# Graph network on one Trainium2 core: scatters without an index limit, and another order in the prologue

## What is computed

```
h = relu(layernorm(x))
hW = (h @ W.T) as 4 heads of 32;  att[e] = leaky_relu(a_src . hW[src] + a_dst . hW[dst], 0.2)
x = x + segment_sum(att[e] * hW[src], dst)                       # layer 0
h = relu(layernorm(x))
z = concat(h[src], h[dst], edge_attr)
x = x + segment_sum(relu(z @ W_weight + b) * sigmoid(z @ W_gate + b), src)   # layer 1
```

## Time and profile before

| | |
|---|---|
| median of 3 runs | 5451.1 us (5448.32 to 5451.26) |
| profiled execution, whole | 5452.95 us |
| profiled execution, first to last instruction | 5451.3 us |
| granted TensorE clock, mean | 0.897 |
| busy PE / DVE / ACT / POOL | 3900.8 / 3303.6 / 2039.0 / 3655.4 us |

### The profile page before, as it was taken

One profiled execution on the slowest core, in us unless ns is written; L12 is line 12 of the kernel. 1 busy time (PEld: TensorE's weight loads), 2 busy tenths in 40 slices (PEclk: granted clock), 3 DMA queues, 4 the chain that ended last, 5 costly groups with the idle time before them and its releaser, 6 DMA issues.

```text
span 5451.3 us, 120513 instructions
## 1 busy us (share of the span) xinstructions
PE 3900.8 (72%) x33107; PEld 3037.0 (56%) x33107; DVE 3303.6 (61%) x7367; ACT 2039.0 (37%) x4548; POOL 3655.4 (67%) x3908
## 2 busy tenths in 40 slices
PE   5666666666666656698778778877887775888882
PEld 4355555555555555466556556655665554666662
DVE  6999777777777777652222222222222226999996
ACT  4022222222222222353333333333333335888872
POOL 4677777777777777447777777777777774444441
PEclk8898888888888888899999999999999998999996
DMA  5233333333333332465555555555555558999998
GB/s 179 64 81 81 78 76 76 78 76 79 75 76 78 76 78 75 151 226 170 165 164 166 167 167 164 165 166 167 165 165 165 167 161 254 322 324 322 322 315 312
DMA packets 457999, 866.30 MB, mean 159 GB/s; under 512 B 122766, under 2 KB 276056, under 8 KB 457700
## 3 DMA queue, kind: packets, MB, share of 16 engines
q1 hardware_dynamic: 215031, 439.00, 26.2%
q0 software_dynamic: 177312, 379.95, 24.4%
q10 hardware_dynamic: 65620, 46.95, 2.6%
HBM read 558.92 MB, written 313.00 MB: 160 GB/s over the span
## 4 chain that ended last, share of the span: by engine, by line
POOL 45%; issue 20%; DMA 15%; DVE 7%; PE 6%; ACT 3%; POOLq 2%; SPq 1%; ACTq 0%; DVEq 0%
POOL parts L606 20%; POOL gat L588 13%; POOL rows L588 13%; DMA parts<-rows,sidx 7%; DMA rows<-parts 6%; DVE gat L1595 2%; ACT rows L1061 2%; PE ps L679 1%; PE ps L724 1%; DVE msg L1603 1%; PE ps L886 1%; PE ps L845 1%; PE ps L899 1%; POOLq L606 1%; PE ps L848 1%
## 5 line engine op out<-in xcount | busy, mean ns | idle before, releaser
L606 POOL DMA_INDIRECT parts<-rows,sidx x1664 | 1638.5, 985 | 519.1 <-issue 447.0
L768 PE MATMUL ps<-msg,to_node 128*128 128x128 f32 x3328 | 619.1, 363 | 737.1 <-DVE msg L1465 737.1
L845 PE MATMUL ps<-w_edge,gat 128*128 128x256 f32 x3328 | 1057.9, 401 | 1.0 <-ACT hot L1048 1.0
L768 PEld LDWEIGHTS ps<-msg,to_node 128*128 128x128 f32 x3328 | 572.6, 268 | 758.8 <-issue 758.8
L588 POOL DMA_INDIRECT gat<-table,sidx x832 | 793.9, 954 | 272.8 <-issue 269.1
L588 POOL DMA_INDIRECT rows<-table,sidx x832 | 791.6, 951 | 253.6 <-issue 250.2
L1061 ACT ACTIVATE rows<-ps 128x512 f32<-128x512 f32 x832 | 453.5, 600 | 1352.7 <-DMA parts<-rows,sidx 1266.0
L1553 DVE COPY rows<-srcf 128x8 f32 (+1 forms) x208 | 42.3, 204 | 1456.1 <-DMA parts<-rows,sidx 1456.1
L848 PE MATMUL ps<-hot,to_edge 128*128 128x256 bf16 x4992 | 855.7, 282 | 0.0
L1033 ACT ACTIVATE earlier<-ps,less_three 128x512 bf16<-128x512 f32 x416 | 263.0, 683 | 1202.6 <-PE ps L777 1140.4
L848 PEld LDWEIGHTS ps<-hot,to_edge 128*128 128x128 bf16 x4992 | 507.3, 102 | 291.8 <-issue 34.8
(11 more groups left out here) (235 smaller groups left out, 6927.2 us busy)
## 6 DMA issues: line engine op xcount, KB each, us to landing
rows<-parts SPq DMA_DIRECT2D x208, 1028.0 KB, 7.6
ea<-in_edge_attr SPq DMA_DIRECT2D x422, 256.0 KB
nodes_w<-table_b SPq DMA_DIRECT2D x208, 128.0 KB
parts<-rows,sidx POOLq DMA_INDIRECT x1664
nodes_w<-table_a SPq DMA_DIRECT2D x416, 64.0 KB, 5.2
gat<-table,sidx POOLq DMA_INDIRECT x832
rows<-table,sidx POOLq DMA_INDIRECT x832
x1w<-x ACTq DMA_DIRECT2D x208, 64.0 KB
```

Source lines behind the costliest of these rows:

```text
L606: nc.gpsimd.indirect_dma_start(out=parts, out_offset=bass.IndirectOffsetOnAxis(ap=sidx[:, s, j:j + 1], axis=0), in_=rows[:, s, j, :], in_o ...
L768: mmi = pe.matmul(out_ps, to_node[:, s % 2, j * P:(j + 1) * P], msg[:, s % 2, j * F:(j + 1) * F], start=(j == 0), stop=(j == J - 1))
L845: pe.matmul(z, eat[:, s % 2, j // 4, (j % 4) * P:(j % 4 + 1) * P], w_edge[:], start=True, stop=False)
```

## The change

- The scatters lose `bounds_check` and `oob_is_err`.
- SP issues the ten copies of x to x1 behind `nodes_done` and the `ids` loads, and waits for `windows_known` 2 before the last loop.
- PE's 32 transposes of the ids and ACT's eight evictions stand behind the first four node steps.
- DVE runs `group_windows` before the last of the node steps, and `keys` is split: `ids_of_gathers` and `key_of(0)` behind the last node step, `key_of(1)` behind the first eight `next_gather`.
- The masks for the histogram (`hist_masks`, L1371 to 1380) stand between the last two `split_scores`.
- The counting by source and `passes2` (L1403 to 1422, L1424), with PE's matmul, stand between the first loop and `nodes(1)`.
- PE and ACT wait for `windows_known` 1 before the first loop, and they and POOL for 2 before the last.

```diff
@@ sync @@
-                if layer == 0:
-                    for k in range(LAST):
-                        sp.dma_start(last_rows(x1, k), last_rows(x, k)).then_inc(x_copied, 16)
                 sp.wait_ge(nodes_done, layer + 1)
...
+            for k in range(LAST):
+                sp.dma_start(last_rows(x1, k), last_rows(x, k)).then_inc(x_copied, 16)
             passes = sp.value_load(passes_i[0:1, 0, 2:3], min_val=1, max_val=WINDOWS)
@@ gpsimd @@
                             nc.gpsimd.indirect_dma_start(
                                 out=parts, out_offset=bass.IndirectOffsetOnAxis(ap=sidx[:, s, j:j + 1], axis=0),
-                                in_=rows[:, s, j, :], in_offset=None,
-                                bounds_check=(G + 1) * GE - 1, oob_is_err=True,
-                            ).then_inc(placed[s], 16)
+                                in_=rows[:, s, j, :], in_offset=None).then_inc(placed[s], 16)
@@ tensor @@
+            def turn_ids():
+                pe.wait_ge(node_out, XU + 1)
+                pe.wait_ge(node_ht, XU + 1)
+                for k, (g0, n) in enumerate(CH):
+                    for s in range(2):
+                        pe.wait_ge(real_up, 2 * k + s + 1)
+                        for j in range(J):
+                            mmi = pe.transpose(ps[:, 4 * k + 2 * s + j // 4, (j % 4) * P:(j % 4) * P + n],
+                                               prep_real(k, s)[0:n, j * P:(j + 1) * P], ident[0:n, 0:n])
+                        mmi.then_inc(turned, 1)
+                pe.wait_ge(idx_up, 4 * len(CH))
...
                         node_products(layer, s, s)
+                    turn_ids()
                     limits()
...
-            pe.wait_ge(counted_up, 1)
-            pe.matmul(ps[:, 2, 0:KH], ones[:], counted[:, 1, :], start=True, stop=True).then_inc(counted_ps, 1)
-            pe.wait_ge(windows_known, 2)
+            pe.wait_ge(windows_known, 1)
...
+            pe.wait_ge(counted_up, 1)
+            pe.matmul(ps[:, 2, 0:KH], ones[:], counted[:, 1, :], start=True, stop=True).then_inc(counted_ps, 1)
             nodes(1)
@@ scalar, nodes @@
+                turned_out(layer, 0, 0)
                 if layer == 0:
+                    for s in range(XU):
+                        step(s, 0, s)
                     ids_out()
-                turned_out(layer, 0, 0)
-                with act.Fori(0, T // XU - 1) as i:
+                with act.Fori(0, T // XU - 2 + layer) as i:
                     for s in range(XU):
-                        step(XU * i + s, i, s)
+                        step(XU * (i + 1 - layer) + s, i + 1 - layer, s)
@@ vector, nodes @@
-                if layer == 0:
-                    group_windows()
-                    keys()
                 for s in range(XU):
                     step(T // XU - 1, s, ahead=min(3, XU - s))
+                    if layer == 0 and s == XU - 2:
+                        group_windows()
                 if layer == 0:
+                    ids_of_gathers()
+                    key_of(0)
                     split_scores(T - 2, (T - 2) % XU)
+                    hist_masks()
                     split_scores(T - 1, (T - 1) % XU)
...
             for s in range(V):
                 next_gather(s, s)
+            key_of(1)
```

More of the change, by code:

```diff
@@ L434, in _ @@
                 sp.sem_inc(pass_done[1], 1)
+            sp.wait_ge(windows_known, 2)
             passes2 = sp.value_load(passes_i[0:1, 1, 2:3], min_val=1, max_val=2 * WINDOWS)
@@ L613, in _ @@
             pool.sem_inc(all_placed, 1)
+            pool.wait_ge(windows_known, 2)
             passes2 = pool.value_load(passes_i[0:1, 1, 2:3], min_val=1, max_val=2 * WINDOWS)
@@ L648, in _ @@
             pe.wait_ge(w_sb, 3)
[L650 to L657, removed]
             def node_turned(layer, t, s):
@@ L868, in _ @@
                     edge_products(s, q, q + w, GU - 1)
+            pe.wait_ge(windows_known, 2)
             passes2 = pe.value_load(passes_i[0:1, 1, 2:3], min_val=1, max_val=2 * WINDOWS)
@@ L1011, in _ @@
             act.wait_ge(nodes_done, 1)
-            act.wait_ge(windows_known, 2)
+            act.wait_ge(windows_known, 1)
             passes = act.value_load(passes_i[0:1, 0, 2:3], min_val=1, max_val=WINDOWS)
@@ L1083, in _ @@
                     evict_rows(s, q, turn, True)
+            act.wait_ge(windows_known, 2)
             passes2 = act.value_load(passes_i[0:1, 1, 2:3], min_val=1, max_val=2 * WINDOWS)
@@ L1216, in group_windows, with ids_of_gathers @@
                 passes_of(0, span[:, 0:G], 7)
-            def keys():
+            def ids_of_gathers():
                 dve.wait_ge(idx_up, 4 * len(CH))
@@ L1221, in keys, with key_of, hist_masks @@
                 link(nc.vector.tensor_copy(src_i[:, G:G + V, :], srcf[:, 0:V, :]))
+            def key_of(d):
                 low = prep_low.rearrange("p (g j) -> p g j", j=J)
[L1223 to L1226, removed]
+                if d == 0:
+                    link(nc.vector.tensor_scalar(low, src_i[:, 0:G, :], 9, None, ALU.arith_shift_right))
+                else:
+                    link(nc.vector.tensor_scalar(low, src_i[:, 0:G, :], 4, B - 1, ALU.arith_shift_right,
+                                                 ALU.bitwise_and))
+                link(nc.vector.tensor_copy(key[:, 0:G, d, :], low))
+            def hist_masks():
+                link(nc.vector.tensor_copy(digit_i[:, 0:1], iota_p[:]))
+                link(nc.vector.tensor_scalar(digit_i[:, 1:2], digit_i[:, 0:1], J - 1, None, ALU.bitwise_and))
+                link(nc.vector.tensor_copy(digit[:, 2:3], digit_i[:, 1:2]))
+                link(nc.vector.tensor_scalar(digit_i[:, 1:2], digit_i[:, 0:1], 3, None, ALU.arith_shift_right))
+                link(nc.vector.tensor_copy(digit[:, 0:1], digit_i[:, 1:2]))
+                link(nc.vector.tensor_scalar(digit[:, 1:2], digit[:, 0:1], float(B // 2), None, ALU.add))
+                for h in range(2):
+                    link(nc.vector.tensor_scalar(same[:, h, :], iota_m[:].rearrange("p r n -> p (r n)"),
+                                                 digit[:, h:h + 1], None, ALU.is_equal))
+                link(nc.vector.tensor_scalar(iota_u, iota_u, digit[:, 2:3], None, ALU.is_equal))
             def take_stats(layer, t, i, s):
@@ L1370, in _ @@
                     one_hot_once(s, U * i + s).then_inc(hist_hot, 1)
[L1371 to L1380, removed]
             dve.wait_ge(hist_ps, G + U + 1)
@@ L1401, in _ @@
             link(nc.vector.tensor_scalar(run0[:], total[:, 4, :], float(LOW // 2), None, ALU.add))
[L1403 to L1421, removed]
-            passes_of(1, spans, 6)
             passes = dve.value_load(passes_i[0:1, 0, 2:3], min_val=1, max_val=WINDOWS)
-            passes2 = dve.value_load(passes_i[0:1, 1, 2:3], min_val=1, max_val=2 * WINDOWS)
             link(nc.vector.tensor_copy(start[:], base[:]))
@@ L1521, in _ @@
                 dve.wait_ge(spread_up[0], (w + 1) * (G + 1))
+            part = B // 4
+            for r in range(4):
+                ins = nc.vector.tensor_copy(ends_of[r * B:(r + 1) * B, :],
+                                            total[r * B:(r + 1) * B, 3, r * part:(r + 1) * part])
+                ins.then_inc(prep_dve, 1)
+            step[0] += 4
+            dve.wait_ge(prep_dve, step[0])
+            link(nc.vector.tensor_scalar(counted[:, 0, :], place[:], ends_of[:, 0:1], None, ALU.is_ge))
+            for b in range(1, part):
+                link(nc.vector.scalar_tensor_tensor(counted[:, b % 2, :], place[:], ends_of[:, b:b + 1],
+                                                    counted[:, (b - 1) % 2, :], ALU.is_ge, ALU.add))
+            assert part % 2 == 0
+            dve.sem_inc(counted_up, 1)
+            dve.wait_ge(counted_ps, 1)
+            link(nc.vector.tensor_scalar(start_src[:], ps[:, 2, 0:KH], float(NODES_IN_BUCKET), None, ALU.mult))
+            spans = prep_tmp[:, 0:2 * G]
+            link(nc.vector.tensor_scalar(spans, start_src[:, 1:2 * G + 1], float(NODES_IN_BUCKET - 1), float(N - 1),
+                                         ALU.add, ALU.min))
+            link(nc.vector.tensor_tensor(spans, spans, start_src[:, 0:2 * G], ALU.subtract))
+            passes_of(1, spans, 6)
+            passes2 = dve.value_load(passes_i[0:1, 1, 2:3], min_val=1, max_val=2 * WINDOWS)
             nodes(1)
```

## The result

The changed kernel takes 5400.6 us in the median of five runs (5398.61 to 5401.57) against 5451.1 before (five runs here, 5448.32 to 5452.6): 50.5 us less. The ratio of the medians is 0.9907; the ratio on record is 0.9901, with a 95% interval of 0.9884 to 0.9918. The profiled execution spans 5399.5 us instead of 5451.3, at a mean granted clock of 0.902 (0.897 before). The forecast was 5362. On one of the chips of the experiments a run of the kernel before took 9007.43 us; it was in the slow state and is left out of the comparison there.

A forecast was written before the change was run, and what follows sets the result against it. POOL's back-to-back issue of gathers and scatters was taken as the bound. Prologue -29.1, limit -60.5 and counting +0.5 sum to -89.1 us, giving 5362 from the 5451.1 median; own spread 5348 to 5380, wider range 5346 to 5424.

The forecast's parts named there:

- Ids: Prologue: transposes and evictions leave the start for a gap behind four node steps; 7.3 us gained, range 5.3 to 7.3.
- Histogram: DVE in the prologue: histogram starts 15.0 us earlier, at 108, from ids and from windows and keys.
- 2.3 + 11.8: DVE's path behind the histogram start: masks leave for 2.3 us, source counting with a register load for 11.8.
- rival 3: Prologue: copies of x queue behind the ids load and come late, losing 24 of 29 us; 5386, chance 0.05.
- Rival 5: Prologue's gain does not pass: POOL's first 64 gathers start no earlier or DVE's order stalls; 5391, chance 0.04.
- the step on windows and keys: DVE before the histogram: 7.9 us block returns in pieces filling idle time once copies leave; 7.9 less 0.2 us gained.
- The counting behind the loop: DVE after the first loop: counting of 11.8 to 12.7 us fits a 12.0 us wait; cost 0.5 us.
- The limit: POOL's 1664 scatters: without the check each costs 36.4 ns less, like a gather; 60.5 us gained.
- (1): Scatters: limit is free, the 38 ns are the scatter's three packets; 5422, chance 0.15; half case 5392, chance 0.08.
- (2): Scatters: the MOVE before each was not hidden, so 67 ns each, 111 us, are gained; 5311, chance 0.04.
- (4): Scatters without a limit take a slower path, costing 68 us more; 5491, chance 0.03.
- What would show it: Expected signs: scatters of 0.945 to 0.95 us, histogram at 108, POOL's restart at 204; 0.98 would mean the limit is free.

The follow-up runs named there:

- e8: Changed kernel with PE's id transposes and ACT's evictions back ahead of the first node tile; 5404.73 us against 5452.98 for the kernel before.
- e7: Changed kernel with the counting by source and PE's matmul back ahead of the first loop; 5426.52 us against 5462.94 for the kernel before.
- e6: Changed kernel with the ten copies of x to x1 back before nodes_done; 5420.75 us against 5462.94 for the kernel before.
- e1: Kernel before with only the scatters' limit taken off; 5428.46 us against 5451.12.
- e5: Changed kernel with scatters moving 128 of 257 floats per row into a table of their own; 5399.11 us in one run.
- e4: Changed kernel with a limit put on the gathers; 5499.97 us against 5451.12 for the kernel before.
- e9: Changed kernel with scatters moving 128 of 257 floats into their own table, and the limit back on them; 5423.78 us in one run.
- e3: Changed kernel with scatters moving 256 of 257 floats per row into a table of their own; 5399.07 us in one run.
- e2: Changed kernel with the limit put back on the scatters; 5420.37 us, ratio 0.9940 to the kernel before.
- e12: Changed kernel with counting behind the second loop, four x tiles loaded earlier, three DVE operations moved into waits; 5402.7 us against 5462.94.

## Why the prediction was right, and where it was wrong

**The bound and the prologue: right, nearly to the step.** Forecast 29.1 us at POOL's restart, measured 29.5. Ids: forecast 7.3, measured 8.1 in the trace, and 6.9 to 8.2 at the restart alone in e8. Their return into the gap: fits, as said; PE's transposes took 4.74 us there, not 8.3 (the granted clock was 0.64 in this stretch and 0.50 in the row from which they were priced). Histogram: forecast 108, measured 107.7. Behind it, forecast 2.3 + 11.8 = 14.1, measured 13.7, and e7 gives 11.4 to 12.0 for the counting, against 11.8. First gather forecast 111.4, measured 111.3; restart 204.3 and 203.9, with 8 and 7.35 us of idle before it. The ids' last packet starts at 153.0 (forecast: near 153) and the copies are complete at 170.3 (within 20 us more), beside gathers and at the old 20 GB/s, so rival 3 is out. Rival 5 is out by the restart. What the step on windows and keys did not price by itself is the copies: e6 shows 8.1 to 9.1 of the 15.7 us hanging on them.

**The counting behind the loop: forecast 0.5, measured 0.** The x tile landed 1.08 us after DVE was free.

**The limit: the mechanism right, the size wrong.** The term that failed is "I take the row it is nearest to, the gather: 36.4 ns, 60.5 us". Measured are 13 ns and 21.6 us (22.7 in e1). The 39 us between are the whole error: 5362 + 39 = 5401. The gather row was no picture of a scatter without a limit, for two reasons that no row of before shows. 24 of the 37 ns between the two are there with no limit at all, and 22 of them with the gather's number of packets too (e5), and what the limit itself costs depends on the direction: 13 ns on a scatter, 63 on a gather (e4, e9). Of the rivals, (1) had the right thought, that most of the difference is the scatter's own, and the wrong cause: three packets, refuted by e5. Its count was off as well: one of the three, and one of the gather's two, has 4 bytes, so it is two packets of data against one (e3). It gave 5422 for none of the gain and 5392 for half; a third of it came. (2) is out, the MOVE was hidden (e2), and (4) is out, the pitch fell.

**What would show it** was written as a choice between 0.945 and 0.98; the reading was 0.972, which is neither. Of the total, the forecast's own spread (5348 to 5380) missed, while the range that took in rival 1 held the time. It held because it reached up to rival 1, not because the step on the limit was right.

## What to carry to other kernels

When an operation appears in a trace only with its option on, the nearest other operation gives a bound, not a price: here forecast and outcome differ by a factor of three, and one experiment that takes the option away, or puts it on the other operation, costs less than the argument. Time moved out of a prologue passes whole as long as the engine that sets the pace still waits for it: look at its idle time at the restart (7.35 us are left here). A block may move for nothing into a wait that a load sets, but it then hides that load: move the load ahead next.

## What the runs showed of the hardware that was not expected

- A limit on the indices costs an indirect DMA of 128 rows 63 ns if the list is on the read side (0.947 to 1.010 us) and 13 ns if it is on the write side (0.971 to 0.984), whatever its value (12627 or 214015).
- An indirect scatter of 128 rows takes POOL 22 to 24 ns longer than a gather (0.947), with rows of 512, 1024 or 1028 bytes (0.969, 0.971, 0.971).
- Whole rows go together into a packet of some 4 KB: eight of 528 or of 512 bytes (4224, 4096), four of 1028 or of 1024 (4112, 4096). The queue's count has one packet of 4 bytes per engine and transfer beside these.
- POOL's own speed differs between executions. In e7 and e12 the gathers have a pitch of 1.260 us (medians of 0.956) and the scatters one of 1.279 and 1.280; in e6's profiled run, on the same chip, it is 1.254 (0.947) and 1.276. The median overstates the difference: single gathers lie near 0.945 or near 0.953 to 0.956 us, and e8 has a median of 0.952 for half of its gathers at a pitch of 1.255. By the pitches 1600 gathers and 1664 scatters cost 12.7 us more in e7 and 15.2 in e12 than in e6. The profiled run of e6 took 5403.27 us, its three others 5420.06 to 5421.98, 17 to 19 more. These have no profile, so that it is the same cause is argued only. Why POOL is slower in one execution stays open.
